# DMA transposes for the quantized patches of groups 2 to 8 and for the gate/up weights, and a feed-forward part written out, in a ViT layer kernel

## The reference, cut to what matters

```python
# tokenizer: patches normalised, quantized per token, times a ternary weight
xn = patches * rsqrt(mean(patches**2) + 1e-6)
s  = 127 / clip(max(|xn|), 1e-5)
h  = concat(cls, (clip(round(xn * s), -128, 127) / s) @ wq.T) + pos
# attention, three scales with weights of their own (16 heads of 16, causal), then Wout and a LayerNorm
h  = h + attention(layernorm(h))
# feed-forward (I = 704), fake quantization with one step over the whole tensor
y    = act_quant(layernorm(h), clip_x)            # needs max |.| over all tokens
gate = y @ wquant(w_gate).T ; up = y @ wquant(w_up).T
a    = act_quant(silu(gate) * up, clip_down)      # again a max over all tokens
h    = h + a @ wquant(w_down).T
```

## Time and profile before

| | us |
|---|---|
| median of 3 runs | 777.65 (776.64 to 777.92) |
| the profiled execution | 776.94 |
| its span | 775.1 |
| PE busy | 686.7 (89%) |
| VectorE busy | 645.5 (83%) |
| ScalarE busy | 582.4 (75%) |
| GpSimd busy | 523.8 (68%) |

### The profile page before, as it was taken

The page is one execution under the profiler, slowest core; times in us unless marked ns, Lnnn a source line. Parts: engine busy times, 40 slices in busy tenths (PEclk is TensorE's granted clock), DMA queues, the critical chain, the costliest instruction groups (busy, mean ns, idle before and its releaser), DMA issues. The chain is left out here.

```text
span 775.1 us, 26199 instructions
## 1 busy us (share of the span) xinstructions
PE 686.7 (89%) x9862; PEld 536.8 (69%) x9862; DVE 645.5 (83%) x1396; ACT 582.4 (75%) x1278; POOL 523.8 (68%) x791
## 2 busy tenths in 40 slices
PE   0498899999999999999999999999999999378674
PEld 0277678777877777878877877788788777244363
DVE  4788876899889988989898889889886997769957
ACT  3567878778788678869777877788778886379593
POOL 3449965957686859877677888388848886521174
PEclk9979999999999999999999999999999999879878
DMA  8301000000010000101000000000000000000014
GB/s 236 100 29 33 17 18 4 32 18 19 1 34 22 15 3 32 34 2 33 18 18 3 18 18 12 25 24 32 19 3 22 20 21 21 1 1 0 1 40 129
DMA packets 14958, 21.91 MB, mean 28 GB/s; under 512 B 1972, under 2 KB 11446, under 8 KB 14840
## 3 DMA queue, kind: packets, MB, share of 16 engines
q1 hardware_dynamic: 14404, 19.91, 8.4%
q10 hardware_dynamic: 436, 0.40, 0.2%
HBM read 17.03 MB, written 3.28 MB: 26 GB/s over the span
## 5 line engine op out<-in xcount | busy, mean ns | idle before, releaser
L904 POOL TENSOR_TENSOR k_bd<-kT,rmask 128x400 f32<-128x400 f32 x192 | 167.7, 901 | 7.4 <-PE ps_s L1357 4.3
L805 ACT COPY pT<-ps_w 25x400 f32<-25x400 f32 x192 | 94.6, 493 | 9.3 <-PE ps_w L1372 6.7
L1398 PE MATMUL ps_w<-oy_hi,o_hi 128*128 128x512 f32 x192 | 94.9, 494 | 0.0
L913 POOL TENSOR_TENSOR prob_hi<-prob_hi,rsum 128x800 f32<-128x800 f32 x48 | 74.8, 1558 | 13.4 <-DVE rsum L1150 13.3
L1133 DVE TENSOR_REDUCE nmax<-ps_s 128x16 f32<-128x400 f32 x96 | 72.4, 766 | 11.5 <-PE ps_s L1357 11.3
L785 ACT COPY v_bd<-ps_w 50x256 f32<-50x256 f32 x192 | 70.3, 366 | 13.3 <-PE ps_w L1332 10.9
L1398 PE MATMUL ps_w<-oy_hi,o_lo 128*128 128x512 f32 x192 | 76.3, 397 | 0.0
L1398 PE MATMUL ps_w<-oy_lo,o_hi 128*128 128x512 f32 x192 | 76.2, 397 | 0.0
L826 ACT ACTIVATE ps_w<-ps_w 128x256 f32<-128x256 f32 x96 | 35.7, 372 | 51.8 <-PE ps_w L1398 50.4
L918 POOL TENSOR_TENSOR ln<-ln,ln_eps 128x1 f32<-128x1 f32 x96 | 20.0, 208 | 75.2 <-ACT ps_w L826 74.8
L1357 PE MATMUL ps_s<-k_bd,qT 64*25 64x200 f32 (+1 forms) x3072 | 70.5, 291 | 0.0
(11 more groups left out here) (235 smaller groups left out, 2080.2 us busy)
## 6 DMA issues: line engine op xcount, KB each, us to landing
x_in<-in_x SPq DMA_DIRECT2D x64, 147.0 KB
out<-hidden SPq DMA_DIRECT2D x16, 200.0 KB
pT<-in_tok_w SPq DMA_DIRECT2D x1, 768.0 KB, 6.6
hidden<-in_wq SPq DMA_DIRECT2D x1, 768.0 KB, 8.9
k_bd<-in_wk SPq DMA_DIRECT2D x1, 768.0 KB, 9.4
v_bd<-in_wv SPq DMA_DIRECT2D x1, 768.0 KB, 9.0
hidden<-in_wout SPq DMA_DIRECT2D x1, 768.0 KB, 9.0
hidden<-in_wo SPq DMA_DIRECT2D x1, 768.0 KB, 10.8
```

Source lines behind the costliest of these rows:

```text
L805: last = nc.scalar.copy(pT[ROWB * h:ROWB * h + LQ, s % 2, c::2, :, 0:LQ], ps_w[row:row + LQ, bank].rearrange("p (j t) -> p j t", j=4)[:, : ...
L904: last = nc.gpsimd.tensor_tensor(k_bd[:, v % KBD, c], kT[:, w % 2, c, 2 * p * L:(2 * p + 2) * L].unsqueeze(1).broadcast_to([P, HR, 2 * L]) ...
L913: nc.gpsimd.tensor_tensor(pr, pr, rsum[:, s % 2, e].unsqueeze(2).broadcast_to([P, H, WIDTH[e]]), ALU.mult).then_inc(prob_ready, 1)
L1398: mm = nc.tensor.matmul(G[:], ot[:, s % 2, c, 2 * (p % 2):2 * (p % 2) + 2].rearrange("p b t -> p (b t)"), wt[:, w, c], start=False, stop=( ...
```

## The change

1. For pairs 4 to 31 and chunks 0 to 3 the transposes of x_q leave TensorE and the copies leave ScalarE. SyncE issues one transposing DMA each, from x_q in SBUF into x_qT or wgT in SBUF (32 in all, of 128 x 768 bf16). It waits for x_q and for the embed matmuls of the pair before. VectorE's next x_q and TensorE's embed wait for the DMA (`xqT_turned`). Pairs 0 to 3 stay as they were. In the tables of ScalarE and TensorE the steps that stay keep their order, only their ticks are renumbered; those of VectorE and GpSimd are not touched; SyncE's has, after the loads for pair 6, a transposing step and a load in turn.
2. Feed-forward: the loops are written out; two memsets go from VectorE to GpSimd; -mean*rstd is computed ahead, so that one tensor_scalar gives both columns of `tok`; GpSimd casts y of groups 0 and 1 before w_down, and VectorE casts half of group 0; w_down is turned at the end of the gate/up phase, and ScalarE copies it.
3. Down phase: VectorE scales in place in PSUM and adds from PSUM to `hidden` (no o_s); TensorE's reuse of the PSUM half waits for the add instead of the scaling; the last group is scaled, added and stored in two halves.

```diff
+                if kind == "turn_d":
+                    n = PAIRS + step[1]
+                    c = ffn_chunk(n // PAIRS, n % PAIRS)
+                    sp.wait_ge(xq_ready, n + 1)
+                    if c is None:
+                        bank, fill = bank_of(("embed", (n - 1) % PAIRS, (n - 1) // PAIRS))
+                        sp.wait_ge(filled[bank], fill)
+                        dst = x_qT[:]
+                    else:
+                        dst = wgT[:, c // 2, 3 * (c % 2):3 * (c % 2) + 3].rearrange("p f k t -> p (f k) t")
+                    sp.dma_start(dst, x_q[:], transpose=True).then_inc(xqT_turned, 16)
...
-                    c = ffn_chunk(m, p)
-                    if c is not None:
-                        w_ps = ps_w[:, bank, 0:PC * P // 2].bitcast(BF16)
-                        dst = wgT[:, c // 2, 3 * (c % 2):3 * (c % 2) + 3].rearrange("p f k t -> p (f k t)")
-                        nc.scalar.copy(dst, w_ps).then_inc(xqT_ready, 1)
-                        return
...
-                    need(dve, xqT_ready, n)
+                    need(dve, xqT_ready, min(n, PAIRS))
+                    need(dve, xqT_turned, 16 * (n - PAIRS))
                     nc.vector.tensor_scalar(x_q[:], x_t[:], MAGIC, None, ALU.subtract).then_inc(xq_ready, 1)
...
-                    pe.wait_ge(xqT_ready, PAIRS * m + p + 1)
+                    if m == 0:
+                        pe.wait_ge(xqT_ready, p + 1)
+                    else:
+                        pe.wait_ge(xqT_turned, 16 * (PAIRS * (m - 1) + p + 1))
...
+            for k, bank in enumerate((3, 0)):
+                act.wait_ge(wd_turned, k + 1)
+                nc.scalar.copy(wdT[:, :, k * P:(k + 1) * P],
+                               ps_w[:, bank].bitcast(BF16)[:, 0:FC * P].rearrange("p (f t) -> p f t", f=FC)).then_inc(wd_ready, 1)
...
+            y_cast(0, PAIRS // 2)
+            y_cast(1)
             pool.wait_ge(wint_ready, KC)
             nc.gpsimd.tensor_copy(w_q[:, :, 0:I], w_int[:]).then_inc(wq_ready, 1)
...
-            nc.vector.tensor_scalar(tok[:, 2], rstd, mx[:, 4:5], None, ALU.mult).then_inc(y_ready, 1)
-            dve.wait_ge(y_ready, 1)
-            nc.vector.scalar_tensor_tensor(tok[:, 3], mean, -1.0, tok[:, 2], ALU.mult, ALU.mult).then_inc(y_ready, 1)
+            dve.wait_ge(dev_chain, 4)
+            nc.vector.tensor_scalar(tok[:, 2:4], norm3[:], mx[:, 4:5], None, ALU.mult).then_inc(y_ready, 1)
...
             y_ints3(0, 0, 2)
+            dve.wait_ge(yint3_ready, 1)
+            nc.vector.tensor_copy(y_q[:, 0, :, PAIRS // 2:].rearrange("p k q t -> p q k t"),
+                                  y_int[:, 0, PAIRS // 2:].rearrange("p q (k t) -> p q k t", k=KC)).then_inc(first_q, 1)
             y_ints3(1, 1)
...
+            def scaled(g, r, first=0, pairs=PAIRS):
+                ps = down_ps(r)[:, first:first + pairs]
+                nc.vector.scalar_tensor_tensor(ps, ps, sg[:, 1, 0:1], drow[:].unsqueeze(1).broadcast_to([P, pairs, D]),
+                                               ALU.mult, ALU.mult).then_inc(down_scaled, 1)
+                dve.wait_ge(down_scaled, g + first // 2 + 1)
+                h = hidden[:, g * PAIRS + first:g * PAIRS + first + pairs, :]
+                nc.vector.tensor_tensor(h, h, ps, ALU.add).then_inc(result_ready, 1)
...
+            pe.wait_ge(silu_ready, GROUPS * FC - 2 + 3)
+            turn_wd(1, 0)
             find_max(1)
+            pe.wait_ge(wd_ready, KC)
...
-                    pe.wait_ge(down_read, g - 1 + T)
+                    pe.wait_ge(result_ready, g - 1 + T)
```

More of the change, by code:

```diff
@@ L1402, in layer @@
     att.close()
+    T = 2
     tok = sb(ffn, "tok", [P, 4, NPAIR])
@@ L1467, in _ @@
         def _(sp):
-            with sp.Fori(0, GROUPS) as g:
-                sp.wait_ge(result_ready, g + 1 + T)
+            pieces = [(g * PAIRS, PAIRS) for g in range(GROUPS - 1)] + [(NPAIR - PAIRS, PAIRS // 2), (NPAIR - PAIRS // 2, PAIRS // 2)]
+            for i, (n, pairs) in enumerate(pieces):
+                sp.wait_ge(result_ready, i + 1 + T)
                 for row, b in HALVES:
-                    sp.dma_start(out[bass.ds(g * GB, GB)].rearrange("(q two) t d -> two t q d", two=2)[b],
-                                 hidden[row:row + L, bass.ds(g * PAIRS, PAIRS), :]).then_inc(stored, 16)
-            sp.wait_ge(stored, 32 * GROUPS)
+                    sp.dma_start(out[2 * n:2 * (n + pairs)].rearrange("(q two) t d -> two t q d", two=2)[b],
+                                 hidden[row:row + L, n:n + pairs, :]).then_inc(stored, 16)
+            sp.wait_ge(stored, 32 * (GROUPS + 1))
         @block.scalar
@@ L1509, in _ @@
             act.wait_ge(step_chain, 3)
-            with act.Fori(0, GROUPS // 2 - 1) as g2:
+            for g2 in range(GROUPS // 2 - 1):
                 for r in (0, 1):
@@ L1523, in _ @@
                         y_out(1, GROUPS - 1)
+            for k, bank in enumerate((3, 0)):
+                act.wait_ge(wd_turned, k + 1)
+                nc.scalar.copy(wdT[:, :, k * P:(k + 1) * P],
+                               ps_w[:, bank].bitcast(BF16)[:, 0:FC * P].rearrange("p (f t) -> p f t", f=FC)).then_inc(wd_ready, 1)
             act.wait_ge(hstep_chain, 4)
-            with act.Fori(0, GROUPS // 2) as g2:
+            for g2 in range(GROUPS // 2):
                 for r in (0, 1):
@@ L1537, in _, with y_cast @@
             pool.sem_inc(yq_ready, T)
+            nc.gpsimd.memset(mx[:], 0.0).then_inc(f_zeroed, 1)
+            nc.gpsimd.memset(one_f[:], 1.0).then_inc(f_zeroed, 1)
             nc.gpsimd.memset(w_q[:, :, I:], 0.0).then_inc(f_zeroed, 1)
+            def y_cast(g, pairs=PAIRS):
+                pool.wait_ge(yint_ready, g + 1)
+                if g > 0:
+                    pool.wait_ge(yint3_ready, g + 1)
+                pool.wait_ge(yT_filled, g - 1 + T)
+                nc.gpsimd.tensor_copy(y_q[:, g % 2, :, 0:pairs].rearrange("p k q t -> p q k t"),
+                                      y_int[:, g % 2, 0:pairs].rearrange("p q (k t) -> p q k t", k=KC)).then_inc(yq_ready, 1)
+            y_cast(0, PAIRS // 2)
+            y_cast(1)
             pool.wait_ge(wint_ready, KC)
             nc.gpsimd.tensor_copy(w_q[:, :, 0:I], w_int[:]).then_inc(wq_ready, 1)
-            for g in range(GROUPS):
-                pool.wait_ge(yint_ready, g + 1)
-                pool.wait_ge(yint3_ready, g + 1)
-                pool.wait_ge(yT_filled, g - 1 + T)
-                nc.gpsimd.tensor_copy(y_q[:, g % 2].rearrange("p k q t -> p q k t"),
-                                      y_int[:, g % 2].rearrange("p q (k t) -> p q k t", k=KC)).then_inc(yq_ready, 1)
+            for g in range(2, GROUPS):
+                y_cast(g)
             nc.gpsimd.memset(h_q[:, :, :, :, L:], 0.0).then_inc(f_zeroed, 1)
@@ L1639, in _ @@
             nc.vector.tensor_scalar(hcol[:, 2], gu_scale[:, FC:], mx[:, 5:6], None, ALU.mult).then_inc(hstep_chain, 1)
-            def scaled(g, r):
-                dve.wait_ge(down_filled, g + 1 + T)
-                nc.vector.scalar_tensor_tensor(o_s[:, r], down_ps(r), sg[:, 1, 0:1], drow[:].unsqueeze(1).broadcast_to([P, PAIRS, D]),
-                                               ALU.mult, ALU.mult).then_inc(down_read, 1)
-                dve.wait_ge(down_read, g + 1 + T)
-                h = hidden[:, bass.ds(g * PAIRS, PAIRS), :]
-                nc.vector.tensor_tensor(h, h, o_s[:, r], ALU.add).then_inc(result_ready, 1)
-            with dve.Fori(0, GROUPS // 2) as g2:
-                for r in (0, 1):
-                    scaled(g2 * 2 + r, r)
+            def scaled(g, r, first=0, pairs=PAIRS):
[5 more added lines that the diff above has]
+                nc.vector.tensor_tensor(h, h, ps, ALU.add).then_inc(result_ready, 1)
+            for g in range(GROUPS - 1):
+                dve.wait_ge(down_filled, g + 1 + T)
+                scaled(g, g % 2)
+            dve.wait_ge(half_filled, 1)
+            scaled(GROUPS - 1, 1, 0, PAIRS // 2)
+            dve.wait_ge(down_filled, GROUPS + T)
+            scaled(GROUPS - 1, 1, PAIRS // 2, PAIRS // 2)
         @block.tensor
@@ L1695, in _, with turn_wd @@
             pe.wait_ge(drow_filled, 2)
-            pe.wait_ge(wq_ready, 1)
-            pe.wait_ge(f_zeroed, 3)
-            for k in range(KC):
+            def turn_wd(k, bank):
+                pe.wait_ge(wq_ready, 1)
+                pe.wait_ge(f_zeroed, 3)
                 for f in range(FC):
-                    mm = nc.tensor.transpose(ps_s[:, 1, k].bitcast(BF16)[:, f * P:(f + 1) * P], w_q[:, k, f * P:(f + 1) * P], id16[:])
+                    mm = nc.tensor.transpose(ps_w[:, bank].bitcast(BF16)[:, f * P:(f + 1) * P], w_q[:, k, f * P:(f + 1) * P], id16[:])
                 mm.then_inc(wd_turned, 1)
             turn_y(0, 0)
-            with pe.Fori(0, GROUPS // 2 - 1) as g2:
+            for g2 in range(GROUPS // 2 - 1):
                 for r in (0, 1):
@@ L1713, in _ @@
                         turn_y(1, GROUPS - 1)
```

(9 more changed lines are left out.)

134 lines of the change are left out of this document (67 added, 67 removed), and 62 rows, old and new, of the table AT.

## The result

The changed kernel takes 781.81 us (median of 20 runs, 778.07 to 787.98) beside 776.95 (median of 20 runs, 773.37 to 782.11) of the kernel before on the same chip: ratio 1.0069, interval 1.0048 to 1.0091. It is slower by 0.7%; the forecast was 766, with a range of 755 to 776 and a gain. Its profiled execution took 779.67 us with a span of 777.9 and lies 2.1 us under the median of its 20 runs; before's 776.94 lies on the median of its 20. So the two traces differ by 2.8 us in the span, the medians by 4.9.

What follows compares the result with a forecast made beforehand. The prediction took TensorE, 98% busy in attention, to set the pace, with VectorE and ScalarE bounding the feed-forward phases. Its terms, -14.1 + 8 - 1.5 - 4.2 = -11.8 us, gave 766 us, range 755 to 776.

Steps and rivals of the forecast that it cites:

- (a): Attention and weight chunks: TensorE loses 32 transposing steps of 0.44 us each, all won as time, -14.1 us.
- TensorE's freed time is not won: Rival: VectorE's chain and one-buffer waits take over, half of the 14.1 us stays; 773 us, chance 0.12.
- (b): Attention: VectorE's next x_q and TensorE's embed wait for transposing DMAs of 4.5 to 5.5 us at short places, +8 us.
- (c): SyncE's queue: 32 more issues hold no load longer, and the four weight DMAs have over 10 us each; 0.
- (e): Feed-forward loops written out: groups already follow each other without a gap on VectorE; 0.
- (d): Start of the feed-forward: shorter tok, first cast halved and shared, first y transposes earlier, -1.5 us.
- (f): Down phase: adds from PSUM take 1.23 us, ScalarE then sets the pace, last store halved; -4.2 us.
- the 5.7: The gain forecast for the feed-forward, its start (-1.5) and down phase (-4.2) together.
- only rival on the slower side: Rival: a transposing DMA takes 8 us, so its waits cost +30 instead of +8; 788 us, chance 0.13.
- PE between two groups' starts about 1.8 us less: Sign expected in the changed kernel's profile: TensorE's distance between group starts shrinks by about 1.8 us, before stalls.

Runs made afterwards that it cites:

- the DMA part alone: Kernel before with only the hunks of the transposing DMAs, its feed-forward part kept: 788.34 us, ratio 1.0144.
- the second tiles: Whole change plus a second tile for x_q and x_qT, used by odd pairs of groups 3 to 8, own semaphore for odd DMAs: 782.31 us, ratio 1.0055.
- the kernel with three cuts and no turning: Kernel before with max/min (VectorE), square (ScalarE) and b2 addition (GpSimd) over fewer columns, patches of groups 2 to 8 not turned: 771.1 us, ratio 0.9911.
- the first pairs on TensorE: Whole change, but the first pair of each of groups 2 to 8 turned on TensorE and copied by ScalarE as before: 772.5 us, ratio 0.9948.

## Why the prediction was wrong, step by step

- **(a), the step that failed: "TensorE sets the pace, and what leaves it there is time won", -14.1.** Leaving the same work out altogether (28 of the 32 steps) gave 1.0003, doubling it 1.0018. PE's 98% in the earlier trace rows is a share of overlapping, modelled records. It said that PE has something to do, not that others wait for it. The part of the new idle time that the trace names is mostly at the transposes of the probabilities (1.4 us before, 5.6 after). The rival "TensorE's freed time is not won" named the cause, but let half of the gain stand (773); nothing of it did. What does set the pace stays open: no cut gave back much more than a third of what it took off (5.1 of 14.0 us at most).
- **(b), +8: right in size, +9.3 measured, in part by luck.** PE's waits were forecast as 3.1 at pair 12, 2.25 at pair 24, 1.0 at pair 27 and 0.4; they were 3.10, 3.56, 0.21 and none. The sum, 6.9 against 6.75, is right because the misses cancel. Where the DMA was waited for it took 5.2 us from the end of x_q at pair 12 (5.5 forecast) and 6.6 at pair 24. VectorE's own waits were 12.5 us where 4 were forecast as VectorE's alone; 2 us of cost were forecast for them, and the trace shows some 1.4. The three steps of the ln2 start, 3.0 + 4.4 + 1.4 = 8.8, account for the 9.3. What the forecast lacked is the clock. Where it stays at 1.00 behind a wait, the step is as long as the wait (3.0 for 3.10 in the kernel after, 2.7 for 2.75 in the DMA part alone, both at pair 12). Where it falls, the step is longer by 0.7 to 2.1 us (4.4 for 3.56 here, 5.2 for 3.23 and 3.9 for 3.18 with the second tiles, 5.3 for 3.23 in the DMA part alone).
- **(c), (e), 0:** the kernel with two pairs turned as before has the feed-forward part's time, so the 26 other patch DMAs and the 4 of weights cost nothing that these runs can tell. (e), the loops, was not run by itself.
- **(d) and (f), -1.5 and -4.2.** The start gained 1.56 and the last add moved 3.2 us towards ACT's end, as forecast; the stage lost 6.2 us in the trace. The runs give 3.9 (2.3 to 5.6) for this part; the 5.7 is just outside, and why the runs give less than the two traces is not shown.
- **The sum.** With (a) at 0, (b) at +9.3 and the feed-forward at -3.9 the change is +5.4 us, which is 1.0069; it must come out, since the 9.3 was taken as the difference. Had (a) alone been set to 0, the forecast's own terms would have given +2.3, the right direction. The forecast's only rival on the slower side (788) had a transposing DMA of 8 us as its reason; the longest took 5.8, the median 3.8. So the chance of 0.13 for a slower kernel stood on another mechanism than the one that came.
- Of what was to show in the profile, this came: waits for the DMA on PE near 7 us in sum, 24 records of the old transposes left, adds at 1.2 us, ACT without a pause, DVE's end 3 us nearer. Three things did not: the landing was to take 4.5 to 5.5 us and took 3.8 at the median (2.8 to 5.8), PE was to wait in four to six places and waited in three, and "PE between two groups' starts about 1.8 us less" was not there, and on it hung the sign.

A part of the profiled difference stays aside: at the border to the feed-forward the ln2 step jumps by 2.8 us in the kernel after, against before. In the fourteen other kernels it jumps by 1.3 to 2.7 against before, with one exception (-0.1), the kernel with three cuts and no turning. Before and that kernel are the only two profiles whose granted clock stays at 1.00 over the ten us that begin just in front of this step's last three; the others have means of 0.72 to 0.83. So it seems to be before's profiled execution that was fast there, and the jump no cost of the change. The last stretch of 10 us at the border, first before, then after:

```profile
657.00:667.00 10.00, 6.41 (x98) 4.72 (x96) 7.70 (x22) 5.34 (x14) 5.28 (x14) 1.00 0.01 2
```
```profile
666.00:676.00 10.00, 7.09 (x78) 4.77 (x78) 6.47 (x20) 2.39 (x8) 3.67 (x9) 0.66 0.01 2
```

The version that is best of these is any with the feed-forward part and without the two long waits: the feed-forward part alone (0.995), with the first pairs on TensorE (0.9948) and with pairs 12 and 24 on TensorE (0.9946) can't be told apart. All three beat both kernels.

## What to carry to other kernels

Before freed time on a "98% busy" engine is priced, leave that work out and time the kernel: here 12.3 us of TensorE work were worth 0, and 45 us at another place a quarter. Price a new wait the other way round, place by place, from the distance between producer and first user on the engine whose order the rest follows: two waits of 3 us at 2 of 28 places cost most of 9.3 us, while 12.5 us of waits on the engine beside it cost some 1.5. Look at the granted clock behind each wait: here it added up to two thirds of the wait's length. A transfer that replaces on-chip work is then best used where the distance is long, and the old way kept at the few short ones.

## What the runs showed of the hardware that was not expected

- A transposing DMA of 128x768 bf16 between SBUF buffers holds SP's issue for 1.21 us and lands after 2.8 to 5.8 us, 3.8 at the median; 801 packets at 33 ns of queue time each. The Trainium skill's page VectorE: DVE Perf Modes, section The three transpose paths, gives 1309 ns for one 128x128 block; six in a row would be an estimate of 7.9 us, and the measured 3.8 for six blocks says that they don't go one after another at that price.
- VectorE's add of 128x1024 with one operand in PSUM took 1.22 us throughout while GpSimd cast, where the add of two SBUF operands took 1.90.
- TensorE waited 3.56 us at pair 24 and had a granted clock of 0.50 (1.2 GHz) from 451 to 453 us behind it; the wait of 3.56 us then cost 4.4. After the wait of 3.10 us at pair 12 the clock was 1.00 and the cost 3.0. In the kernel with the second tiles the wait at pair 12 was 3.23 us, the clock 0.50 from 217 to 223 us and the cost 5.2.
